# Modulation rows first, then spread over the partitions: another order of an attention-and-experts kernel's opening

## The reference

```
mod = (silu(c) @ wmod).reshape(4, 6, 1, 512)      # c: 4 x 512, wmod: 512 x 3072
sa, ca, ga, sb, cb, gb = mod[:, 0], ..., mod[:, 5]
ga, gb = sign * max(abs, 0.25) of themselves
h = layernorm(x) * (1 + ca) + sa
x = x + ga * attn(h)      # rmsnorm * gamma, projection to q, kv, a (512 x 1536),
                          # scan along the tokens: s = sigmoid(a) * s + kv, result q * s
h = layernorm(x) * (1 + cb) + sb
x = x + gb * ffn(h)       # 8 experts, top 2, capacity 320 a batch, two layers of width 2048
```

## Time and profile before

| | us |
|---|---|
| three runs | 2194.17, 2195.23, 2197.80 |
| median | 2195.23 |
| the profiled execution | 2202.21 |
| its span | 2200.5 |
| TensorE busy | 2157.7 |
| VectorE busy | 1600.8 |
| ScalarE busy | 1031.0 |
| GpSimd busy | 365.9 |

### The profile page before, as it was taken

The page is one execution under the profiler, slowest core; times in us unless marked ns, Lnnn a source line. Parts: engine busy times, 40 slices in busy tenths (PEclk is TensorE's granted clock), DMA queues, the critical chain, the costliest instruction groups (busy, mean ns, idle before and its releaser), DMA issues.

```text
span 2200.5 us, 33604 instructions
## 1 busy us (share of the span) xinstructions
PE 2157.7 (98%) x12538; PEld 1186.4 (54%) x12538; DVE 1600.8 (73%) x2850; ACT 1031.0 (47%) x2042; POOL 365.9 (17%) x334
## 2 busy tenths in 40 slices
PE   7999999999999999999999999999999999999997
PEld 2454444445464646556564655556464655656463
DVE  6799999989884487587668758775875787487341
ACT  5466666666370535255253615534461644356050
POOL 0124343343323010100101010110101010000101
PEclk9999999999999999999999999999999999999999
DMA  7799996765765344344525443452444355333301
GB/s 268 246 241 247 241 249 156 182 166 126 162 174 157 95 118 140 89 116 110 144 77 126 133 102 108 118 149 72 98 140 115 100 130 142 84 101 97 44 6 24
DMA packets 350883, 296.73 MB, mean 135 GB/s; under 512 B 242331, under 2 KB 242331, under 8 KB 350208
## 3 DMA queue, kind: packets, MB, share of 16 engines
q1 hardware_dynamic: 328960, 252.44, 41.7%
q0 software_dynamic: 21760, 42.14, 10.2%
HBM read 159.64 MB, written 93.01 MB: 115 GB/s over the span
## 4 chain that ended last, share of the span: by engine, by line
PE 92%; DVE 3%; SPq 2%; issue 1%; DMA 1%; ACT 1%; POOL 0%; DVEq 0%; ACTq 0%; POOLq 0%
PE bank L1974 37%; PE bank L1915 28%; PE bank L1831 20%; PE bank L1903 4%; PE bank L1786 1%; PE bank L1749 1%; SPq L483 0%; SPq L473 0%; PE bank L1742 0%; DMA reg_d<-in_wmod 0%; DMA reg_e<-reg_e 0%; DMA mod_rows<-reg_a 0%; DVE reg_b L1438 0%; DVE mxw L1157 0%; DVE reg_e L1536 0%
## 5 line engine op out<-in xcount | busy, mean ns | idle before, releaser
L1974 PE MATMUL bank<-reg_b,reg_c 128*128 128x512 f16 x3840 | 831.7, 379 | 1.0 <-DVE reg_b L1438 1.0
L1974 PEld LDWEIGHTS bank<-reg_b,reg_c 128*128 128x128 f16 x3840 | 375.6, 98 | 452.0 <-issue 1.9
L1831 PE MATMUL bank<-reg_c 128*128 128x512 f16 x2304 | 508.8, 380 | 1.9 <-DMA reg_c<-reg_a 1.8
L1915 PE MATMUL bank<-reg_e,reg_a 128*128 128x320 f16 x2688 | 417.6, 299 | 0.0
L1831 PEld LDWEIGHTS bank<-reg_c 128*128 128x128 f16 x2304 | 223.3, 98 | 262.2 <-issue 5.3
L1915 PEld LDWEIGHTS bank<-reg_e,reg_a 128*128 128x128 f16 x2688 | 262.2, 98 | 105.2
L736 POOL DMA_INDIRECT out_dram<-reg_e,midx x80 | 139.7, 1746 | 1014.7 <-DVE reg_e L1460 901.9
L1456 DVE SCALAR_TENSOR_TENSOR reg_e<-bank,inv,reg_e 128x512 f32<-128x512 f32 x80 | 59.8, 748 | 263.0 <-PE bank L1974 263.0
L947 ACT ACTIVATE reg_e<-bank,b1s 128x320 f32<-128x320 f32 x112 | 59.0, 527 | 394.0 <-PE bank L1915 394.0
L1915 PE MATMUL bank<-reg_e,reg_d 128*128 128x320 f16 x1344 | 216.9, 299 | 0.0
L1915 PEld LDWEIGHTS bank<-reg_e,reg_d 128*128 128x128 f16 x1344 | 130.3, 98 | 53.8 <-ACT reg_e L947 3.8
(11 more groups left out here) (231 smaller groups left out, 2601.2 us busy)
## 6 DMA issues: line engine op xcount, KB each, us to landing
reg_d<-in_w SPq DMA_DIRECT2D x224, 512.0 KB, 4.2
slot_rows<-zrow SPq DMA_DIRECT2D x32, 516.0 KB, 4.8
reg_b<-in_x SPq DMA_DIRECT2D x16, 1024.0 KB, 7.4
out_dram<-reg_b SPq DMA_DIRECT2D x16, 1024.0 KB, 7.6
reg_d<-in_w SPq DMA_DIRECT2D x8, 1024.0 KB, 9.5
slot_rows<-zrow SPq DMA_DIRECT2D x32, 129.0 KB, 4.7
reg_d<-in_wmod SPq DMA_DIRECT2D x4, 1024.0 KB, 14.5
reg_e<-mod_rows SPq DMA_DIRECT2D x7, 512.0 KB, 10.3
```

The costliest lines, as they stand in the source:

```text
L1831: ins = mm(dst[:, :], wqs[:, ws, kc, e0:e0 + P], xns[:, j % 2, xs, kc, :], start=kc == 0 and xs == 0 and ws == 0, stop=kc == KC - 1 and ws ...
L1915: ins = mm(dst[:, 0:CAP], w[ws][:, c, p * P:(p + 1) * P], xs_of[:, KC * xs + 2 * i + c, j * CAP:(j + 1) * CAP], start=first and c == 0 and ...
L1974: ins = mm(bank_y[i % 2][:, :], hid[:, hs, hc, t * P:(t + 1) * P], w2s[:, ws, hc, :], start=k == 0 and hs == 0 and ws == 0, stop=k == HC - ...
```

## The change

Only the opening and the first projection group are touched.

- All six modules are made by `mod_mm` as four rows. For modules 1 and 0, batch 0's row is then spread by one product with a row of ones as weights (contraction 1, 128 columns) and copied out of its bank. Module 1's row is taken out of its bank, with 1 added, by VectorE; module 0's by ScalarE. `silcb` is gone.
- SyncE's loads come as: module 1, x of block 0, module 0, wq 0, wq 1, module 2, wq 2, module 3, wq 3, modules 4 and 5, x of block 1.
- TensorE has modules 2 and 3 ahead of the maxima's transposition, 4 and 5 behind the maxima's product.
- VectorE's second apply comes after the first of wq's maxima instead of the second. Two of block 0's four low halves are put between the steps of the maxima.
- The first projection group does its eight products with wq's high halves first, each part as its high half is there, then the four with the low halves.
- Counts of waits follow; SyncE gets a wait for module 1's row ahead of a later write.

```diff
-MOD_DONE = {1: 1, 0: 2, 2: 5, 3: 6, 4: 7, 5: 8}
-ROW_DONE = {0: 3, 1: 4, 2: 5, 3: 6, 4: 7, 5: 8}
+ROW_DONE = {1: 1, 0: 2, 2: 3, 3: 4, 4: 5, 5: 6}
...
-            load_x(0, 0)
...
             load_wmod(1)
+            load_x(0, 0)
             load_wmod(0)
-            for c in range(KC):
-                sp.dma_start(wq_raw[:, c, :], wq[c * P:(c + 1) * P, :]).then_inc(s_wqraw[c], 16)
+            load_wq(0)
+            load_wq(1)
+            load_wmod(2)
+            load_wq(2)
+            load_wmod(3)
+            load_wq(3)
+            load_wmod(4)
+            load_wmod(5)
             load_x(0, 1)
-            for m in range(2, 6):
-                load_wmod(m)
...
                     sp.wait_ge(s_dch, 14)
+                    sp.wait_ge(s_mrow1, 1)
...
-            sp.wait_ge(s_modmm, MOD_DONE[5])
+            sp.wait_ge(s_modmm, ROW_DONE[5])
...
             stats1(0, 0)
-            act.wait_ge(s_modmm, MOD_DONE[0])
-            a.activation(mods[:, 0, :], bank[0][:, :], ACT.Copy).then_inc(s_mod0, 1)
...
+            mod_copy(0)
+            act.wait_ge(s_spread, 2)
+            a.activation(mods[:, 0, :], bank[0][:, :], ACT.Copy).then_inc(s_mod0, 1)
             square(0)
             hi1(0)
-            mod_copy(0)
-            mod_copy(1)
...
-            dve.wait_ge(s_silc, 1)
-            v_.tensor_copy(silcb, silc[:, :, 0:1].to_broadcast([P, KC, P])).then_inc(s_silb, 1)
-            dve.wait_ge(s_modmm, MOD_DONE[1])
-            v_.tensor_scalar(mods[:, 1, :], bank[1][:, :], 1.0, None, ALU.add).then_inc(s_modc, 1)
+            dve.wait_ge(s_modmm, ROW_DONE[1])
+            v_.tensor_scalar(modr[0:B, D:2 * D], bank[MOD_BANK[1]][0:B, :], 1.0, None, ALU.add).then_inc(s_mrow1, 1)
+            dve.wait_ge(s_spread, 1)
+            v_.tensor_copy(mods[:, 1, :], bank[1][:, :]).then_inc(s_modc, 1)
...
             wq_max(0)
+            apply1(0, 0, 1)
             wq_max(1)
-            apply1(0, 0, 1)
             wq_max(2)
             wq_max(3)
...
+            lo1(0, 0, 1)
...
+            lo1(0, 1, 2)
...
-            lo1(0)
+            lo1(0, 2, TB)
...
-                wm = stage[:, m, :].rearrange("p (c n) -> p c n", c=KC)
-                pe.wait_ge(s_wmod[m], 16)
-                for c in range(KC):
-                    ins = mm(bank[m][:, :], silcb[:, c, :], wm[:, c, :], start=c == 0, stop=c == KC - 1)
-                ins.then_inc(s_modmm, 1)
+                ins = mm(bank[m][:, :], ones32[0:1, :], modr[0:1, m * D:(m + 1) * D], start=True, stop=True)
+                ins.then_inc(s_spread, 1)
...
-            pe.wait_ge(s_silb, 1)
+            mod_mm(1)
+            pe.wait_ge(s_mrow1, 1)
             mod_spread(1)
+            mod_mm(0)
+            pe.wait_ge(s_modc2, 1)
             mod_spread(0)
-            mod_mm(0)
-            mod_mm(1)
+            mod_mm(2)
+            mod_mm(3)
...
-            for m in range(2, 6):
-                if m == 5:
-                    pe.wait_ge(s_modc, 1)
-                mod_mm(m)
+            mod_mm(4)
+            pe.wait_ge(s_modc, 1)
+            mod_mm(5)
...
+                first = n == 0 and c == 0 and kind == 0
+                if first:
+                    for kc in range(KC):
+                        pe.wait_ge(s_wqhi, kc + 1)
+                        for xs in range(2):
+                            mm(dst[:, :], wqs[:, 0, kc, e0:e0 + P], xns[:, 0, xs, kc, :], start=kc == 0 and xs == 0, stop=False)
                 for kc in range(KC):
-                    if n == 0 and c == 0 and kind == 0:
+                    if first:
                         pe.wait_ge(s_wqlo, kc + 1)
-                    for xs, ws in ((0, 0), (1, 0), (0, 1)):
+                    for xs, ws in ((0, 1),) if first else ((0, 0), (1, 0), (0, 1)):
```

More of the change, by code:

```diff
@@ L126, in build_program @@
         modt = reg_e[:, TB * D:TB * D + 2 * D]
-        silcb = h2T.rearrange("p c n -> p (c n)").bitcast(F32)[:, 0:KC * P].rearrange("p (c n) -> p c n", c=KC)
         at[0] = 0
@@ L265, in build_program @@
         s_mod0 = sem("s_mod0")
-        s_silb = sem("s_silb")
+        s_mrow1 = sem("s_mrow1")
+        s_spread = sem("s_spread")
         s_pm = sem("s_pm")
@@ L459, in load_wmod, with load_wq @@
                 sp.dma_start(dst, wm[:, :, m * D:(m + 1) * D]).then_inc(s_wmod[m], 16)
+            def load_wq(c):
+                sp.dma_start(wq_raw[:, c, :], wq[c * P:(c + 1) * P, :]).then_inc(s_wqraw[c], 16)
             load_wmod(1)
+            load_x(0, 0)
             load_wmod(0)
-            for c in range(KC):
-                sp.dma_start(wq_raw[:, c, :], wq[c * P:(c + 1) * P, :]).then_inc(s_wqraw[c], 16)
+            load_wq(0)
[6 more added lines that the diff above has]
+            load_wmod(5)
             load_x(0, 1)
-            for m in range(2, 6):
-                load_wmod(m)
             def fill(e, b):
@@ L833, in mod_copy @@
                 a.activation(modr[0:B, m * D:(m + 1) * D], bank[MOD_BANK[m]][0:B, :], ACT.Copy,
-                             bias=1.0 if m in (1, 4) else 0.0).then_inc(s_modc2, 1)
+                             bias=1.0 if m == 4 else 0.0).then_inc(s_modc2, 1)
+            mod_copy(0)
+            act.wait_ge(s_spread, 2)
+            a.activation(mods[:, 0, :], bank[0][:, :], ACT.Copy).then_inc(s_mod0, 1)
             square(0)
             hi1(0)
-            mod_copy(0)
-            mod_copy(1)
             act.wait_ge(s_wch0, WQ_LINKS - 4)
@@ L1081, in apply1, with lo1 @@
                                                 ALU.mult, ALU.add).then_inc(s_h1, 1)
-            def lo1(n):
-                for t in range(TB):
+            def lo1(n, t0=0, t1=TB):
+                for t in range(t0, t1):
                     wait(dve, s_xhi, TB * n + t + 1)
@@ L1186, in _ @@
             assert wlinks[0] == WQ_LINKS
-            dve.wait_ge(s_modc2, 3)
+            dve.wait_ge(s_modc2, 2)
             gate(2)
@@ L1190, in _ @@
             shc = modr[0:B, 6 * D:6 * D + 1]
-            dve.wait_ge(s_modc2, 5)
+            dve.wait_ge(s_modc2, 4)
             link(v_.tensor_reduce(mrow[0:B, 0:1], scb, AX, ALU.max, apply_absolute_value=True))
@@ L1360, in step @@
                 if i == 0:
-                    dve.wait_ge(s_modc2, 6)
+                    dve.wait_ge(s_modc2, 5)
                     gate(5)
@@ L1825, in qkv @@
                 if n == 0 and c == 0 and kind == 1:
-                    pe.wait_ge(s_modc2, 6)
+                    pe.wait_ge(s_modc2, 5)
+                first = n == 0 and c == 0 and kind == 0
[4 more added lines that the diff above has]
+                            mm(dst[:, :], wqs[:, 0, kc, e0:e0 + P], xns[:, 0, xs, kc, :], start=kc == 0 and xs == 0, stop=False)
                 for kc in range(KC):
-                    if n == 0 and c == 0 and kind == 0:
+                    if first:
                         pe.wait_ge(s_wqlo, kc + 1)
-                    for xs, ws in ((0, 0), (1, 0), (0, 1)):
+                    for xs, ws in ((0, 1),) if first else ((0, 0), (1, 0), (0, 1)):
                         ins = mm(dst[:, :], wqs[:, ws, kc, e0:e0 + P], xns[:, j % 2, xs, kc, :],
```

## The result

Over 20 runs of each kernel the median went from 2197.07 us to 2192.81 us: 4.3 us less, ratio 0.998 with a 95% interval of 0.9973 to 0.9987 (2.9 to 5.9 us). The forecast was 4.1 us less, to 2191.1 us; the 20 runs of the kernel before have a median 1.8 us above that of the three that the forecast started from. The gain is 0.19% of the time: the interval excludes "no change", but 0.2%, the line that the forecast drew between faster and unchanged, lies in the middle of it.

The account below looks back on a forecast made before the run. TensorE, busy 98% of the span, was taken as the bound, with VectorE right behind; block 1 earlier by 4.7 us (TensorE) and 3.9 (VectorE) left 4.1: 2195.23 - 4.1 = 2191.1 us, range 2187.0 to 2196.0.

Parts of the forecast that it names:

- Module 1: Opening, first modulation row: row there at 15.95, VectorE's first apply at 18.35 where it was 18.03; later by 0.3 us.
- Module 0 and the maxima: Opening: shift ready at 23.55, VectorE stands 0.7 us before its second apply; last reduction at 31.5 us instead of 30.26.
- Row halves and tenth link: Two of block 0's low halves fill VectorE's idle waits; scales at 35.0, tenth link at 49.4, later by 0.2 us.
- TensorE's saving, not kept: First projection group ends at 43.8, against 50.8; 7 us not kept: seventh group at 60.5, block 0 ends 3.9 earlier.
- SyncE's queue: Loads of blocks 2 and 3 at 40 to 43 us; small write landed at 52.3; block 1's rows 4.7 earlier.
- The sum: Start of block 1: TensorE earlier by 4.7 us, VectorE's last work of block 0 by 3.9; 4.1 us survives.
- rival (a): Before the seventh group: clock falls in TensorE's 2.9 us hole, 1.7 to 3.3 us lost; 2193.7 us; chance 0.15.
- (b): Small write to mod_rows: its 7.20 us are its own, only idle time moves; 2195.3 us, 2193.5 with 4.9; chance 0.09.
- (c): Opening: clock stays low from 9.5 us, modules 2 and 3 bar the maxima on TensorE's queue; 2201 us; chance 0.06.
- (d): Opening and write: faster spacing early, no VectorE stall before second apply, write 1.6 us; 5.5 us, 2189.7; chance 0.14.

Follow-up runs that it names:

- second experiment: Kernel before, with SyncE's two small writes issued ahead of the loads of x's blocks 2 and 3; ratio to the kernel before 0.9999 (0.999 to 1.0008).
- early transposes: Changed kernel with block 1's four transposes issued after ten of step 0's sixteen fills; ratio to the kernel before 0.9977 (0.9967 to 0.9986).
- split undone: Changed kernel with the first projection group's twelve products in their old order; ratio to the kernel before 0.9979 (0.9969 to 0.9989).
- halves undone: Changed kernel with block 0's four low halves together again behind the scales; ratio to the kernel before 0.9988 (0.9978 to 0.9999).
- maxima's order undone: Changed kernel with the second of wq's maxima ahead of VectorE's second apply again; ratio to the kernel before 0.9981 (0.9971 to 0.9992).
- early sigmoid: Changed kernel with step 0's second sigmoid ahead of block 1's squares on ScalarE; ratio to the kernel before 0.9988 (0.9979 to 0.9997).
- load order undone: Changed kernel with all of wq and x's block 1 loaded ahead of the weights of modules 2 to 5; ratio to the kernel before 1.0005 (0.9995 to 1.0014).
- loads held back: Changed kernel with SyncE waiting for VectorE's tenth link before loading x's blocks 2 and 3; ratio to the kernel before 1.0013 (1.0004 to 1.0022).

## Why the prediction was right, and where its sizes were off

- *Module 1.* Right: 18.22 measured, 18.35 forecast. Silc was there at 9.98, not 9.43, half a microsecond later than before, since GpSimd's first constants were; the first product took 5.6 us instead of 6.4. The two errors cancel.
- *Module 0 and the maxima.* Right: second apply at 23.50 (23.55), a stop of 0.88 (0.7), last reduction 31.26 (31.3). Modules 2 and 3 were through at 29.7, 1.8 us ahead of the maxima's transposition.
- *Row halves and tenth link.* 49.10 measured, 49.4 forecast. The scales came at 34.6, not 35.0.
- *TensorE's saving, not kept.* Right: first group from 40.17, the seventh at 60.20 after a stop of 2.89 (60.5 and 2.9).
- *SyncE's queue.* The mechanism was right, the term too small: the write took 1.9 us where I had taken 2.3, and was issued at 49.52, not 50.0; 5.5 us at block 1 instead of 4.7. (The bound "1.9 us earlier" for a write of 4.9 us was a slip too: 56.97 less 54.9 is 2.1.) The measured 1.9 agrees with the 2.0 us that the Trainium skill gives as a transfer's fixed cost (DMA: Bandwidth & Descriptors, section on the anatomy of one DMA, two cost components). The page's fit is for transfers that GpSimd issues; this one is SyncE's. What I hadn't seen is that a write merely put first does not shift the 2 MB away (second experiment); my claim that "fills, transposes and landing follow unchanged" holds only because the loads found an empty stretch.
- *The sum.* I held that between VectorE's 3.9 and TensorE's 4.7 something near 4.1 survives. The trace shows leads of 5.5, 5.0, 5.2 and 5.8 us at the turns of blocks 0 to 3, so VectorE, 4.25 us early, did not hold it down; "VectorE as full as it is" was the wrong reason for taking 4.1. The median moved by 4.3 all the same: that the sum came out at the right number is in part luck. The profiled executions don't carry the clock's falls in equal measure: that of the changed kernel shows none in the first 100 us and that of the kernel before one, at 30 us; of the experiments on the changed kernel three show one between 31 and 40 us and two one behind the stop at 60 us. One of 3.4 us costs 1.7. That rival (a), given 0.15, happens in some of the changed kernel's executions and takes a part of its 5.5 us is a guess. Each execution's mean granted clock is on record, to three digits. Ten of the changed kernel's 20 have 0.998 and a median of 2191.4 us, seven have 0.996 and 2193.7, so its time differs by 2.3 us between the two. But among the experiments closest to it in the opening, those with the early transposes, the split undone, the halves undone and the maxima's order undone have a mean clock of 0.9960 to 0.9963 where the kernel before, beside them, has 0.9955 to 0.9958, no lower (the early sigmoid has 0.9963 against 0.9966). So the record doesn't show that lost clock turned the 5.5 us into 4.3; what did stays open.
- *Rivals.* (b) fell with the 1.9 us. (c) is real, as the load order undone shows, and needs no clock that stays low from the start; the changed kernel kept 1.8 us clear of it. (d) came in part, by the write. (a) was seen twice, in the experiments; its price there was 1.7 us, the low end of the 1.7 to 3.3 forecast.

The profiled spans differ by 11.9 us, far more than the medians. Of it, 3.6 us come at 434 us, where the kernel before waited for transposes and ran on at half clock. Its timeline and window there, and the changed kernel's window at the same work:

```profile
434.34 0.24 PE L1797 MATMUL bank<-wrs,reg_e 128*128 128x16 f16 x4 [1.71 <-DMA reg_e<-reg_e]
```

```profile
436.00:440.00 4.00, 4.00 (x12) 1.50 (x11) 3.62 (x14) 0.84 (x2) 0.00 (x0) 0.57 0.81 309
```

```profile
426.00:430.00 4.00, 4.00 (x49) 2.26 (x47) 3.69 (x13) 2.86 (x6) 1.23 (x2) 1.00 1.00 363
```

The lead at the turns goes there from 5.7 to 9.3 us. I don't put it down to the change: five of the ten experiments on the changed kernel have this stop as well, of 0.26 to 1.30 us and without a fall of the clock, and the kernel before with the write first has none. The last 2.6 us of the difference weren't followed up. One profile against one profile would have told a gain of 12.

## What to carry to other kernels

An engine freed early in an opening gains nothing by itself: look for what starts on its last instruction (here 2 MB of loads), and whether that falls into an empty stretch of the DMA engines. Where two ends stand close together at a meeting point, each shortened alone shows next to nothing and both together show what neither did; test them together before giving either up. And a stop that looks harmless can cost more than its length: here 1.7 us of lower clock on top of 2.9.

## What the runs showed of the hardware

A stop of TensorE of 2.7 to 2.9 us was followed by the 1.2 GHz level in some executions and not in others of nearly the same opening: not behind 2.89 us in the changed kernel, nor behind 2.89 and 2.90 in the loads held back and the early transposes, but behind 2.88 and 2.89 us in two other experiments, for 3.4 us each. Nor does the length alone decide: 3.03 us (sigmoid early) and 3.18 us (halves undone) had no fall behind them. The Trainium skill (TensorE: Matmul & The Clock Gate, section on HAM oscillation) describes matmuls that come back at the lower clock after waits for DMA; the stretch behind the 7.20 us wait, a mean clock of 0.57 from 78 to 86 us, agrees. A small write to DRAM takes 1.9 to 2.0 us when nothing stands before it, and 6.7 to 7.2 behind 2 MB.
